# Row maxima of a two-level attention kernel from interleaved, stacked keys in two row groups

## The reference, cut to what matters

```
qh = (q @ Wq + bq) -> 16 heads of 8 features, 64 rows
kh = (kv @ Wk + bk) -> 16 heads of 8 features, 6272 rows
scores = einsum('bhqd,bhkd->bhqk', qh, kh) * scale[0]
attn = softmax(scores)
out = einsum('bhqk,bhkd->bhqd', attn, vh) @ Wo + bo
```

## Time and profile before

| | |
|---|---|
| median of 3 runs | 267.34 us (266.98 to 268.56) |
| the profiled execution | 268.98 us, span 266.9 us |
| granted TensorE clock, mean | 0.967 of full speed |
| TensorE busy | 237.5 us, 89% of the span, 2117 matmuls |
| DVE / ACT / POOL busy | 170.0 / 152.3 / 50.7 us |

### The profile page before, as it was taken

The page is one execution under the profiler, slowest core; times in us unless marked ns, Lnnn a source line. Parts: engine busy times, 40 slices in busy tenths (PEclk is TensorE's granted clock), DMA queues, the critical chain, the costliest instruction groups (busy, mean ns, idle before and its releaser), DMA issues.

```text
span 266.9 us, 5300 instructions
## 1 busy us (share of the span) xinstructions
PE 237.5 (89%) x2117; PEld 143.8 (54%) x2117; DVE 170.0 (64%) x418; ACT 152.3 (57%) x254; POOL 50.7 (19%) x75
## 2 busy tenths in 40 slices
PE   8979896499999997998898999999999998977875
PEld 2424232398884433456588566666666666632334
DVE  4597996999932335262485777777876873055462
ACT  6637997856832774843257665655656566700041
POOL 8885899300000010000140000000000000000030
PEclk9989999869999999999999999999999999998997
DMA  5899100200077300000899999999898996700000
GB/s 129 222 298 436 67 0 2 80 0 1 2 262 293 152 2 0 0 2 0 109 105 121 127 117 125 102 117 111 105 117 96 119 108 194 295 2 0 1 0 7
DMA packets 5663, 26.89 MB, mean 101 GB/s; under 512 B 2083, under 2 KB 2628, under 8 KB 3942
## 3 DMA queue, kind: packets, MB, share of 16 engines
q1 hardware_dynamic: 5638, 26.54, 51.2%
HBM read 16.84 MB, written 0.03 MB: 63 GB/s over the span
## 4 chain that ended last, share of the span: by engine, by line
PE 39%; ACT 5%; DVE 5%; issue 2%; POOL 2%; POOLq 1%; DVEq 0%
PE B L1091 22%; PE A L1091 15%; ACT probs L647 3%; PE B L1429 1%; POOLq L146 1%; ACT moe_w L627 0%; POOL ctxn L459 0%; POOL ctxn L457 0%; POOL rstd L375 0%; POOL probs L454 0%; DVE late L1057 0%; DVE probs L1024 0%; PE B L1521 0%; DVE probs L1019 0%; DVE m L1018 0%
## 5 line engine op out<-in xcount | busy, mean ns | idle before, releaser
L978 DVE TENSOR_REDUCE mx<-B 128x1 f32<-128x512 f32 (+1 forms) x104 | 65.0, 656 | 17.6 <-PE B L1091 17.0
L647 ACT ACTIVATE probs<-A 128x896 f32<-128x896 f32 x56 | 50.6, 917 | 26.4 <-PE A L1091 26.1
L375 POOL TENSOR_TENSOR rstd<-ve,mhalf 64x1 f32<-64x1 f32 x9 | 5.4, 603 | 188.3 <-DVE ve L684 181.5
L1091 PE MATMUL B<-probs,scores 128*32 128x128 f32 x736 | 34.0, 280 | 2.5 <-ACT probs L647 2.5
L1091 PE MATMUL A<-ctxT,qq 97*128 97x512 f32 (+1 forms) x52 | 25.1, 630 | 2.4 <-DMA ctxT<-in_ctxT 1.6
L1091 PE MATMUL B<-scores,moe_w 128*128 128x512 bf16 (+1 forms) x96 | 26.0, 354 | 0.4 <-DVE mx L978 0.4
L1091 PEld LDWEIGHTS B<-probs,scores 128*32 128x32 f32 x736 | 19.0, 109 | 10.0 <-ACT probs L647 5.8
L742 DVE MAX8 mid<-scores 128x8 f32<-128x196 f32 x64 | 17.9, 348 | 3.8 <-ACT scores L495 3.8
L1091 PEld LDWEIGHTS A<-ctxT,qq 97*128 97x128 f32 x52 | 10.2, 208 | 17.8 <-issue 9.2
L1091 PE MATMUL A<-moe_w 112*128 112x128 bf16 (+2 forms) x146 | 18.4, 267 | 1.4 <-POOL moe_w L445 1.4
L1091 PE MATMUL A<-onec 128*128 128x512 bf16 (+1 forms) x61 | 18.2, 418 | 1.2 <-DVE onec L705 1.2
(11 more groups left out here) (368 smaller groups left out, 371.2 us busy)
## 6 DMA issues: line engine op xcount, KB each, us to landing
ctxT<-scores SPq DMA_DIRECT2D x20, 148.0 KB, 4.7
ctxn<-in_ctxn SPq DMA_DIRECT2D x1, 2352.0 KB, 20.6
moe_w<-in_moe_w SPq DMA_DIRECT2D x1, 2304.0 KB, 8.3
ctxn<-in_moe_w SPq DMA_DIRECT2D x1, 2304.0 KB, 9.3
scores<-in_e_gu SPq DMA_DIRECT2D x1, 2048.0 KB, 7.4
ctxn<-scores SPq DMA_DIRECT2D x10, 148.0 KB, 4.6
moe_w<-scores SPq DMA_DIRECT2D x10, 148.0 KB, 4.8
blob_m<-in_blob_m SPq DMA_DIRECT2D x1, 1467.0 KB, 13.7
```

What stands on the lines that cost most here:

```text
L375: nc.gpsimd.tensor_tensor(rstd[:, :], ve[:, :], mhalf[0:T, :], ALU.pow).then_inc(S["rstd_ready"], 1)
L647: A_(probs[:, (n % RING) * 1024:(n % RING) * 1024 + w], A[:, 2 * (n % 2):2 * (n % 2) + 2, :].rearrange("p a b -> p (a b)")[:, 0:w], ACT.Ex ...
L978: V.tensor_reduce(mx[:, m, t:t + 1], bank[:, 0:SB0[t][1]], AX_X, ALU.max).then_inc(S["max_used"], 1)
L1091: return mm(out_, lhsT, rhs, start=start, stop=stop)
```

## The change

It gives the features a new order on the partitions, and takes the maxima of all pairs but the first from the stacked keys.

- Feature r of pair m lies on partition 8r + m (before: 16m + r). The weights are permuted in the host's layout; the masks and the matrix `rep_q` follow.
- In the stacked keys the copies no longer fill blocks of 16 neighbouring partitions. `SPREAD` gives start row and step: the fill and parts 0, 1, 2 on rows 0, 1, 2, 3 of every four in 0 to 63; part 0 and part 1 alternate in 64 to 95; part 0 in 96 to 111. A copy's source is every eighth partition, its destination every fourth, every second or (the last) every single one. Number and size of the copies stay.
- The first pair's max steps are as before, with `qmax` now for two heads only (128x128 in place of 128x256), placed in `x0T`. The multiplication that made the other pairs' `qmax` (line 990) is gone.
- For pairs 1 to 7 a max step's stationary is `qx` and its moving operand the stacked keys of the pair: rows 0 to 63 on even steps, rows 64 to 95 on odd ones (`MAX_ROWS`). `qx` holds the high part of the queries on those rows that hold the high part of the keys, and zeros elsewhere. Two ACT copies of the form of line 627 make it.
- So tile 0 of pair m now waits for that pair's stack DMAs; the wait for `qmax_sb` 2 is gone.
- SyncE's wait ahead of the last two weight loads is for an earlier step.

```diff
-STACK = [(0, 0), (16, 1), (48, 2), (64, 0), (80, 1), (96, 0)]
+SPREAD = [(0, 4, None), (1, 4, 0), (2, 4, 1), (3, 4, 2), (64, 2, 0), (65, 2, 1), (96, 1, 0)]
+STACK = [(row, step, part) for row, step, part in SPREAD if part is not None]
+MAX_ROWS = [(0, 64), (64, 96)]
...
-                    sp.dma_start(slot[SHIFT_ROW:SHIFT_ROW + PAIR, :], dram["fill"].bitcast(BF16)).then_inc(stack_ld[m % 4], 16)
-                for row, kp in STACK:
+                    sp.dma_start(slot[0:4 * PAIR:4, :], dram["fill"].bitcast(BF16)).then_inc(stack_ld[m % 4], 16)
+                for row, step, kp in STACK:
                     e = K_EARLY * BANK
-                    sp.dma_start(slot[row:row + PAIR, 0:e], early_part[kp][PAIR * m:PAIR * (m + 1), :]).then_inc(stack_ld[m % 4], 16)
-                    sp.dma_start(slot[row:row + PAIR, e:G], kpart[kp][PAIR * m:PAIR * (m + 1), e:G]).then_inc(stack_ld[m % 4], 16)
+                    to = slice(row, row + step * (PAIR - 1) + 1, step)
+                    sp.dma_start(slot[to, 0:e], early_part[kp][m:P:NP, :]).then_inc(stack_ld[m % 4], 16)
+                    sp.dma_start(slot[to, e:G], kpart[kp][m:P:NP, e:G]).then_inc(stack_ld[m % 4], 16)
...
+            act.wait_ge(S["qs_part"], 1)
+            for h in range(2):
+                A_(qx[:, :].rearrange("p (m h t) -> p m h t", h=2, t=T)[:, :, h, :],
+                   qp[:, :].rearrange("p (m t) -> p m t", t=T), ACT.Copy, scale=W["mask_hx"][0:KS, h:h + 1])\
+                    .then_inc(S["qst_ready"], 1)
             evac_values(V_GAP)
...
-            for n in range(4):
-                max_step(n)
-            dve.wait_ge(S["q1_sb"], 1)
-            V.tensor_tensor(qmax[:, 4:H1, :], q1[:, :].unsqueeze(1).to_broadcast([P, H1 - 4, T]),
-                            W["mask_h1"][:, 4:H1].unsqueeze(2).to_broadcast([P, H1 - 4, T]), ALU.mult).then_inc(S["qmax_sb"], 1)
-            for n in range(4, step_at(NP, 0) + 1):
+            for n in range(step_at(NP, 0) + 1):
                 max_step(n)
...
+                elif m == 0:
+                    s, w = SB0[t]
+                    last = one(bank[:, 0:w], qmax[:, :, :].rearrange("p h t -> p (h t)"), key_tile(0, t))
                 else:
+                    if t == 0:
+                        pe.wait_ge(S["qst_ready"], 2)
+                        pe.wait_ge(stack_ld[m % 4], stack_count(m))
                     s, w = SB0[t]
-                    last = one(bank[:, 0:w], qmax[:, 2 * m:2 * m + 2, :].rearrange("p h t -> p (h t)"), key_tile(0, t))
+                    lo, hi = MAX_ROWS[n % 2]
+                    last = one(bank[:, 0:w], qx[lo:hi, m * P:(m + 1) * P], kstack[m % 4][lo:hi, s:s + w])
                 last.then_inc(S["max_ps"], 1)
...
+    w["mask_m"] = p[:, None] % NP == np.arange(NP)
+    spread = PAIR * (np.arange(P) % NP) + np.arange(P) // NP
+    w["wq1"], w["bq1"] = x1["Wq"][:, spread], col(x1["bq"][spread])
```

More of the change, by code:

```diff
@@ L81 @@
           "wq1": (D, D), "rep_q": (P, KS), "wv1": (P, V_ROW), "bq1": (D, 1), "scale1": (P, 1), "wo1": (P, D),
-          "mask_hs": (P, 2), "mask_m": (P, NP), "sel_o": (P, 4 * 9), "wk1": (P, D), "wqT2": (D, D), "wkT2": (D, D), "wvT2": (D, D), "woT2": (T, 2 * D),
+          "mask_hs": (P, 2), "mask_hx": (P, 2), "mask_k1": (P, 2), "mask_m": (P, NP), "sel_o": (P, 4 * 9), "wk1": (P, D), "wqT2": (D, D), "wkT2": (D, D), "wvT2": (D, D), "woT2": (T, 2 * D),
           "causal": (T, T), "mask_p": (P, 2), "wr": (D, 8), "norm_wT": (D, 8)}
@@ L256, in perceiver_kernel @@
         hraw = [hraw0, hraw1]
-        qmax_all, qst_all, v1_rest = carve(moe_w1[:, G // 2:], P, (H1 * T // 2,), (H1 * T // 2,), (3 * V_ROW,))
-        qmax = qmax_all[:, :].bitcast(BF16).rearrange("p (h t) -> p h t", h=H1)
+        qx_all, qst_all, v1_rest = carve(moe_w1[:, G // 2:], P, (H1 * T // 2,), (H1 * T // 2,), (3 * V_ROW,))
+        qmax = x0T[:, :].bitcast(BF16).rearrange("p (h t) -> p h t", h=2)
+        qx = qx_all[0:KS, :].bitcast(BF16)
         qst = qst_all[0:KS, :].bitcast(BF16)
@@ L620, in _ @@
             A_(qs[64:KS, :], A[64:KS, 1, :], ACT.Copy).then_inc(S["qs_part"], 1)
+            act.wait_ge(S["qs_part"], 1)
[3 more added lines that the diff above has]
+                    .then_inc(S["qst_ready"], 1)
             evac_values(V_GAP)
             act.wait_ge(S["qs_left"], 1)
+            act.wait_ge(S["qst_ready"], 2)
             A_(qp[64:KS, :], qrest[64:KS, :], ACT.Copy).then_inc(S["qs_part"], 1)
@@ L943, in _ @@
             dve.wait_ge(S["ld_l"], 16)
-            V.tensor_scalar(hm[:, :], W["mask_h1"], W["scale1"], None, ALU.mult)
+            V.tensor_scalar(hm[:, 0:2], W["mask_k1"], W["scale1"], None, ALU.mult)
             link(V.tensor_scalar(bs[:, :], W["bq1"], W["scale1"], None, ALU.mult))
@@ L973, in max_step @@
                     if shift == 0:
-                        dve.wait_ge(S["qst_ready"], 2)
+                        dve.wait_ge(S["qst_ready"], 4)
                     V.tensor_copy(qst[SHIFT_ROW:SHIFT_ROW + 1, shift * P:(shift + 1) * P], bank[SHIFT_ROW:SHIFT_ROW + 1, 0:P])\
@@ L983, in _ @@
             dve.wait_ge(S["q1_ps"], 1)
-            V.scalar_tensor_tensor(qmax[:, 0:4, :], A[:, 0, 0:T].unsqueeze(1).to_broadcast([P, 4, T]), W["bq1"],
-                                   hm[:, 0:4].unsqueeze(2).to_broadcast([P, 4, T]), ALU.add, ALU.mult)\
+            V.scalar_tensor_tensor(qmax[:, :, :], A[:, 0, 0:T].unsqueeze(1).to_broadcast([P, 2, T]), W["bq1"],
+                                   hm[:, 0:2].unsqueeze(2).to_broadcast([P, 2, T]), ALU.add, ALU.mult)\
                 .then_inc(S["qmax_sb"], 1)
-            for n in range(4):
-                max_step(n)
-            dve.wait_ge(S["q1_sb"], 1)
-            V.tensor_tensor(qmax[:, 4:H1, :], q1[:, :].unsqueeze(1).to_broadcast([P, H1 - 4, T]),
-                            W["mask_h1"][:, 4:H1].unsqueeze(2).to_broadcast([P, H1 - 4, T]), ALU.mult).then_inc(S["qmax_sb"], 1)
-            for n in range(4, step_at(NP, 0) + 1):
+            for n in range(step_at(NP, 0) + 1):
                 max_step(n)
@@ L1397, in _ @@
             pe.wait_ge(S["v1_sb"], len(V_BANKS))
-            pe.wait_ge(S["qmax_sb"], 2)
             NG = len(PACKS)
@@ L1568, in shape_constants @@
     w["rep_q"] = np.zeros((P, KS))
[L1569 to L1572, removed]
+    w["mask_hs"], w["mask_hx"] = np.zeros((P, 2)), np.zeros((P, 2))
+    for row, step, part in SPREAD:
+        for r in range(PAIR):
+            w["rep_q"][NP * r:NP * (r + 1), row + step * r] = 1.0
+            w["mask_hs"][row + step * r, r // DH1] = 1.0
+            if part == 0:
+                w["mask_hx"][row + step * r, r // DH1] = 1.0
+    w["mask_m"] = p[:, None] % NP == np.arange(NP)
+    w["mask_k1"] = (p[:, None] % NP == 0) * (p[:, None] // NP // DH1 == np.arange(2))
     c = p[:, None] % 32
@@ L1612, in lay_out @@
     w["moe_b2"] = np.concatenate([m0["b2"].reshape(-1), m0["sb2"]])
-    w["wq1"], w["bq1"] = x1["Wq"], col(x1["bq"])
-    w["wk1"] = np.concatenate([x1["Wk"], np.zeros((1, D), np.float32), x1["bk"][None]], 0)
+    spread = PAIR * (np.arange(P) % NP) + np.arange(P) // NP
+    w["wq1"], w["bq1"] = x1["Wq"][:, spread], col(x1["bq"][spread])
+    w["wk1"] = np.concatenate([x1["Wk"], np.zeros((1, D), np.float32), x1["bk"][None]], 0)[:, spread]
     parts = []
@@ L1642, in lay_out @@
     out["dft_k"] = w["dft_k"]
-    out["fill"] = np.concatenate([np.full((1, G // 2), 0x3F803F80, np.uint32), np.zeros((15, G // 2), np.uint32)], 0).view(np.float32)
+    out["fill"] = np.where(np.arange(PAIR)[:, None] == SHIFT_ROW // 4, np.full((PAIR, G // 2), 0x3F803F80, np.uint32), np.uint32(0)).view(np.float32)
     c = i["ctx_768"][0]
```

2 lines of the change are left out of this document (1 added, 1 removed).

## The result

The change made the kernel slower: two executions of the changed kernel took 281.0 and 281.3 us, the kernel before 267.64 us as the median of four on the same chip (266.98 to 268.56). The ratio is 1.050 (95% interval 1.045 to 1.056). I had forecast 270.9, with a range of 265.0 to 280.0. Two more executions of the changed kernel took 299.7 and 331.5 us at a lower mean granted clock (0.90 and 0.79, against 0.97) and are left out of the ratio.

The account below looks back on a forecast made before the run. TensorE was taken to bound the loop, VectorE 0.2 us behind and the stacks' transfers as close. 268.98 + 5.6 (waits) - 2.0 (max pairs) = 272.6 us profiled, 270.9 as a median; range 265.0 to 280.0.

Parts of the forecast that it names:

- Part 1, the max pairs: Max pairs in the loop: rows 0-63 and 64-95 run side by side, -0.10 us a full group, -2.0 us in all.
- part 3: First uses of stacks 1 and 2: TensorE stands 2.2 and 3.1 us; everything after runs +5.6 us late.
- The toll: Max pair to score group: a change of the array part in use costs +0.12 us, between 0.10 and 0.16.
- no overlap, and a toll at each change: Max pairs: the two matmuls don't overlap and each change costs 0.12 us; +6.6 us, 279.5 us; chance 0.18.
- Part 2, the copies: Spread stack copies: SyncE issues one every 0.66 us, landing takes 3.9 us, DMA share near 0.6.
- the other branch: Rival on the stack copies: spreading doesn't help, issues stay at 0.97 us, about 290 us; chance 0.07.
- my bound of 0.97: Stack copies: slow bound of SyncE's pace, 11.6 / 12 = 0.97 us an issue.
- The queries' delay ahead of step 13: ACT's two extra copies before the max step that first needs stack 1: a delay of some 0.65 us.
- Stack 3 and the later ones: Later stack copies: stack 3 landed at 170.6, asked for at 172.6, 2 us spare; the later ones gain.
- The clock: Granted clock in the stalls: a fall to 1.2 GHz would add up to 2 us; none counted.

Follow-up runs that it names:

- e3: Changed kernel with rows 0 to 63 for every max step of pairs 1 to 7: 280.7 to 287.3 us.
- e1: Changed kernel with max steps in two groups of 32-row size, rows 64 to 95 and 96 to 111: 275.4 to 285.3 us.
- g1: Changed kernel, pairs 0 to 3 from key parts, 4 to 7 in two 32-row groups, qx made in pass 0: median 267.7 us, ratio 0.990.
- e2: Changed kernel with max steps in two groups of 64-row size, rows 0 to 63 and 64 to 111: 273.5 to 278.4 us.
- f2: Changed kernel with the old feature order and copies of 16 neighbouring partitions to 16 neighbouring ones: 289.9 and 344.4 us.
- e4: Changed kernel with all 112 stacked rows for every max step of pairs 1 to 7: 273.1 to 279.1 us.
- f3: Changed kernel, pairs 0 to 2 from key parts on 128 partitions, pairs 3 to 7 in the 64 and 32 row groups: 278.9 and 317.5 us.
- f4: Changed kernel, pairs 0 to 2 from key parts, pairs 3 to 7 in two 32-row groups: median 270.7 us, ratio 1.000.
- g2: Changed kernel, pairs 0 to 3 from key parts, pairs 4 to 7 in the 64 and 32 row groups: median 272.9 us, ratio 1.013.

## Why the prediction was wrong

**Part 1, the max pairs, is the step that failed.** I had "-0.22 + 0.12 = -0.10 each", on the assumption that rows 0-63 and 64-95 run side by side. Measured: max pair to score group 0.63, +0.20 a group; the 32-row step starts 0.31 behind the 64-row one, so nothing is hidden. The pass was to be 0.34 shorter and is 1.06 longer; over six passes I had -2.0 and got +6.4. That is 8.4 us of the error of 281.0 - 270.9 = 10.1. The rest: 0.9 for the 2.4 us later start less the 1.5 given back at the end, the 1.6 that I had put between profiled execution and median (the changed kernel's was no slower than its like), -0.6 from part 3, and -0.3 between span and device time (2.1 us before, 1.8 now).

The toll itself I had right: 0.10 to 0.16 read from the earlier trace rows, 0.10 measured at each switch, 64 to 128 (e3), 64 to 32 (the changed kernel), 32 to 128 (e1), 128 to 16 (g1). What the earlier trace rows could not show is whether parts of unequal size overlap. I took two equal halves (of the columns, at that) and four equal quarters as evidence for 64 beside 32. The rival "no overlap, and a toll at each change" had it, with +6.6 for the loop and 279.5 us in all; I gave it 0.18. The Trainium skill's "TensorEngine Tiling (Array Packing)" (Tiling Modes, Key Properties), which I cited for it, says that a change of mode drains TensorE; this kernel agrees in that each change of size cost 0.10 us and nothing ran across one, though a drain itself shows in no row. And the Trainium skill's "TensorE: Matmul & The Clock Gate" (Part 3), which speaks of four equal tiles, was no evidence against it: e1 and e2, with two equal tiles each, agree with it, and it says nothing of unequal ones. A sentence that speaks of equal tiles should not have weighed on unequal ones at all.

**Part 2, the copies: right.** SyncE's pace was 0.634 us for most issues and 0.66 over the first 26 with the long one in them (forecast 0.66), the landing of the last copy 3.16 and 3.29 us (forecast 3.9), the DMA share of a pass 0.54 (forecast near 0.6). f2 shows the other branch, at 0.86 an issue: my bound of 0.97 came from dividing a stack's time by 12, where the first four stacks have 13 issues, and the first took 11.08 us, not 11.4 or more. The mechanism that the Trainium skill's "SBUF — State Buffer" (Door 1, the DMA port swizzle) gives is in keeping with it: the same packets took 31.1% of the engines' time instead of 51.2%. By its table of ports I had said too much of the new rows, though: rows 96 to 111 are still 16 neighbours on four ports, so one destination in six gains nothing there. No run tells the ports from another reason.

**Part 3, the waits: right.** +5.05 measured, +5.6 forecast. Idle time was 1.63 and 1.65 us (forecast 2.2 and 3.1): counted from the first fill, both stacks were ready 0.7 us sooner than forecast, and TensorE asked for stack 2 0.9 us later because the tolls slowed pass 0. The queries' delay ahead of step 13 was 0.54 (forecast 0.65): the 0.66 of the two copies less the 0.12 of the narrower `qmax`. Stack 3 and the later ones were in time, as said.

**The clock: not counted, and rightly so for the change's own profile**, which has 1.00 through the loop. It was wrong as a statement about this stage. I had written that nothing in this stage stands still so long. In e1, e2, e3 and e4 waits of 2.3 to 3.5 us at stack 2 went with 6 to 13 us at half clock, beginning in the wait or up to 2.4 us behind it, and this cost e3 5.8 us; I had allowed for up to 2.

## What to carry to other kernels

Before splitting the array by rows, make the parts equal: 64 beside 64 or 32 beside 32 saved 0.12 us of 0.44 a pair here, 32 behind 64 lost 0.20. Count a toll of 0.10 us for every switch between sizes, in and out, and compare it with what one matmul takes; at 0.22 us a matmul, overlapping two leaves little more than half of it. And where an operand moves to a buffer that a DMA queue fills, look at the first uses: keep the old source for the pairs whose copies can't be there yet, since all that the waits cost (5 us here) was lost at the first two.

## What the runs showed of the hardware

- SyncE's own pace bounds the scattered copies: 0.59 us an issue and 0.04 between, whatever the size (48 or 148 KB), but for about one issue in a stack that took 0.9 to 2.2 us in these traces. At a DMA share of 0.54, 16 rows read at every eighth partition and written mostly at every second or fourth land in a median of 2.3 to 2.4 us from issue (48 KB) and 2.6 to 2.7 (148 KB from `scores`); 16 neighbouring ones, with all DMA engines busy, in 4.2 to 4.3 and 4.6 to 4.8.
- A matmul of 512 columns on 16 or 48 rows behaves like one on 32 or 64, one on 112 like one on 128 (rows of e1, e2, e4).
- The two waits of 1.6 us left the clock at 2.4 GHz in the changed kernel's profile. At stack 2 waits of 2.3 to 3.5 us went with 1.2 GHz in all four traces that have them (e1 to e4), while the one of 2.44 us at step 13 in e1 did not. But in f3 a wait of 1.07 us was followed by 1.2 GHz from 171 to 270 us, with TensorE busy 99.0 of these 99 us. Mean clocks of 0.78 to 0.90 were seen in four of the eight executions of kernels with a wait for a stack and the 64 beside 32 rows (the changed kernel, f2, f3); in the 28 with waits and other row groups (e1 to e4, f4) none was under 0.91, and in the four with the mix but no wait (g2) none under 0.96. What brings this on, and why a busy TensorE isn't given its clock back there, stays open.
